# Destination rows of the second edge stage: spans of ranks and a selection on TensorE in place of gathers

## What is computed

```python
src_s = s @ msrc_ws                       # tables per node: TS
dst_s = s @ mdst_ws + mdst_bs             # and TD
ms = src_s[edge_src] + dst_s[edge_dst]    # scalars of an edge
mv = src_v[edge_src] + dst_v[edge_dst]    # vectors of an edge
...
a = jnp.exp(a - amax[edge_dst])           # a weight per edge and head
ns = jax.ops.segment_sum(vs * a[..., None], edge_dst, num_segments=n)
nv = jax.ops.segment_sum(vv * a[..., None, None], edge_dst, num_segments=n)
```

## Time and profile before

| what | value |
|---|---|
| median of 3 runs | 10502.52 us (10501.54 to 10524.19) |
| the profiled execution | 10505.42 us, span 10503.6 us |
| PE busy | 8641.0 us (82%) |
| DVE busy | 7996.0 us (76%) |
| POOL busy | 7636.1 us (73%) |
| ACT busy | 4717.1 us (45%) |
| mean granted TensorE clock | 0.923 of full |

### The profile page before, as it was taken

The page is one execution under the profiler, slowest core; times in us unless marked ns, Lnnn a source line. Parts: engine busy times, 40 slices in busy tenths (PEclk is TensorE's granted clock), DMA queues, the critical chain, the costliest instruction groups (busy, mean ns, idle before and its releaser), DMA issues. The chain is left out here.

```text
span 10503.6 us, 169632 instructions
## 1 busy us (share of the span) xinstructions
PE 8641.0 (82%) x31592; PEld 4931.7 (47%) x31592; DVE 7996.0 (76%) x15399; ACT 4717.1 (45%) x8484; POOL 7636.1 (73%) x5822
## 2 busy tenths in 40 slices
PE   0888888888888799999996888888888887788598
PEld 0444444444444232223233666666666665566333
DVE  3277777777777587888886888888888888888565
ACT  0177666666666311111112444444444444444255
POOL 4488888888888787777785777777777777777332
PEclk9599999999999899999997999999999999999699
DMA  5588888888888899999993444444444444444222
GB/s 202 177 169 168 166 167 166 169 164 172 165 167 168 180 231 225 228 226 229 228 226 90 136 138 136 135 133 139 136 135 135 136 140 135 133 135 137 71 76 58
DMA packets 1075659, 1661.68 MB, mean 158 GB/s; under 512 B 215917, under 2 KB 815288, under 8 KB 1019704
## 3 DMA queue, kind: packets, MB, share of 16 engines
q1 hardware_dynamic: 679744, 1199.16, 41.6%
q0 software_dynamic: 395520, 458.93, 24.5%
HBM read 1483.21 MB, written 443.97 MB: 183 GB/s over the span
## 5 line engine op out<-in xcount | busy, mean ns | idle before, releaser
L436 POOL DMA_INDIRECT sums<-e_total,e_place x1568 | 2481.9, 1583 | 586.3 <-DMA sums<-e_total,e_place 315.7
L1837 POOL DMA_INDIRECT e_rows<-TS,e_at x1568 | 1644.3, 1049 | 567.7 <-issue 451.4
L1837 POOL DMA_INDIRECT e_rows<-TD,e_at x1568 | 1537.3, 980 | 478.0 <-issue 478.0
L573 PE MATMUL ps<-e_win,e_pick 128*128 128x448 f32 x3136 | 1350.6, 576 | 152.9 <-DVE e_u L470 112.4
L1997 PE MATMUL ps<-w_r,e_h 128*128 128x224 f32 x3136 | 840.5, 420 | 424.6 <-DVE e_d L1880 376.1
L573 PEld LDWEIGHTS ps<-e_win,e_pick 128*128 128x128 f32 x3136 | 626.4, 205 | 920.0 <-issue 835.5
L1086 POOL TENSOR_TENSOR n_zv<-n_zv,n_ast 128x1536 f32<-128x1536 f32 x200 | 755.3, 3776 | 410.2 <-DMA n_zv<-in_x_groups 399.3
L1997 PEld LDWEIGHTS ps<-w_r,e_h 128*128 128x128 f32 x3136 | 659.2, 221 | 682.7 <-DVE e_d L1880 558.1
L2006 PE MATMUL ps<-ident,e_d 128*128 128x128 f32 x4704 | 683.6, 283 | 110.1 <-ACT e_dT L2114 108.6
L1266 PE MATMUL ps<-n_z,w_uss 128*64 128x512 f32 x1600 | 742.2, 607 | 26.5 <-DVE n_z L1109 25.8
L2114 ACT ACTIVATE e_oT<-ps 128x512 f32<-128x512 f32 x784 | 468.3, 597 | 628.3 <-PE ps L2032 488.5
(11 more groups left out here) (433 smaller groups left out, 18808.0 us busy)
## 6 DMA issues: line engine op xcount, KB each, us to landing
e_win<-T SPq DMA_DIRECT2D x1568, 168.0 KB
n_z<-in_x_groups SPq DMA_DIRECT2D x400, 512.0 KB
n_zv<-in_x_groups SPq DMA_DIRECT2D x800, 192.0 KB
TOT<-e_tot SPq DMA_DIRECT2D x392, 352.0 KB
e_row<-in_src_rows SPq DMA_DIRECT2D x98, 1024.0 KB
e_row<-in_dst_rows SPq DMA_DIRECT2D x98, 1024.0 KB
e_win<-T SPq DMA_DIRECT2D x1568, 56.0 KB
e_local<-LR SPq DMA_DIRECT2D x98, 512.0 KB
```

What stands on the lines that cost most here:

```text
L436: pool.indirect_dma_start(sums[c], bass.IndirectOffsetOnAxis(ap=place[:, r % 4, c:c + 1], axis=0), total[:, r % 4, c, 0:MSG0], None, compu ...
L573: pe.matmul(g[:, c, :], pick[:, p, R * c:R * c + R], win[:, s, c, :], start=True, stop=True).then_inc(spread, 1)
L1837: pool.indirect_dma_start(rows[:, p, x, c, :], None, table, bass.IndirectOffsetOnAxis(ap=at[:, gp, x, col:col + 1], axis=0)).then_inc(rows ...
```

## The change

TD is now stored by rank instead of by node number: in the node stage GpSimd scatters its rows (place, two scatters in each of the slots 6 and 7, with the rank numbers copied in slot 4), and SP stores only TS. TD gets 128 zero rows more, and baseI is stored to a table BASE, since the tile itself is gone by the second edge stage.

In the second edge stage:

- GpSimd gathers only TS: four indirect DMAs per group. After them it makes the selection e_pick for group i+1 from LR (512 columns, bf16 in, f32 out) and, for group i-8, the weighting e_val (640 columns), which VectorE did before.
- SP loads the windows, four groups ahead: per group eight register loads and eight DMAs on TD, four of them conditional.
- TensorE spreads group i+2: four products of 128 x 160, in two halves, into the two banks that the turns use. Both halves and both turn_backs now stand ahead of weights.
- ScalarE copies both halves (320 columns each) into e_rows.
- VectorE waits for these copies ahead of e_m, and no longer does the weighting.

```diff
-                sp.wait_ge(out_s, 16 * NB)
+                sp.wait_ge(based, 2)
+                sp.dma_start(BASE.rearrange("(a g) c -> a (g c)", a=1), baseI[:].rearrange("a g b c -> a (g b c)")).then_inc(out_s, 16)
+                sp.wait_ge(out_s, 16 * NB + 16)
...
-                    for j, to in enumerate((TS, TD)):
-                        sp.dma_start(to[at, :].rearrange("(t n) w -> n t w", t=2), rows[:, r, :, X * j:X * j + X]
-                                     ).then_inc(stored[r], 16)
+                    sp.dma_start(TS[at, :].rearrange("(t n) w -> n t w", t=2), rows[:, r, :, 0:X]).then_inc(stored[r], 16)
...
+                def ranks(c):
+                    if not c.before(2):
+                        for r in range(2):
+                            gate(pool, k)
+                            pool.wait_ge(placed[r], c.n(32, 0, 1))
+                    pool.tensor_copy(rank_of[:, c.p], rank[:, bass.ds(c.n(4), 4)]).then_inc(ranked, 1)
+
+                def place(c, r):
+                    gate(pool, k)
+                    pool.wait_ge(rows_kept, c.n(2, r + 1))
+                    gate(pool, k)
+                    pool.wait_ge(ranked, c.n(1, 1))
+                    pool.sem_inc(begun, 1)
+                    gate(pool, k)
+                    for j in range(2):
+                        pool.indirect_dma_start(TD, bass.IndirectOffsetOnAxis(ap=rank_of[:, c.p, 2 * r + j:2 * r + j + 1], axis=0),
+                                                rows[:, r, j, X:2 * X], None).then_inc(placed[r], 16)
+
                 def body(g):
                     for s in range(PARTS):
                         vectors(g, s)
                         if s == 1 and g.plus(1).within():
                             add_up(g.plus(1))
+                        if s == 4 and not g.before(1):
+                            ranks(g.plus(-1))
+                        if s >= 6 and not g.before(1):
+                            place(g.plus(-1), s - 6)
 
                 add_up(Group(0, 0))
                 groups(pool, body)
+                ranks(Group(NG // 2, 0))
+                for r in range(2):
+                    place(Group(NG // 2, 0), r)
...
-            return 2 + (5 * i.r + j) % 2
+            return 2 + (7 * i.r + j) % 2
...
+                def load_windows(i):
+                    s = i.r % 4
+                    if s == 0:
+                        sp.sem_inc(asked, 1)
+                        gate(sp, k)
+                        sp.wait_ge(base_here[i.r // 4], i.uses(16, 16))
+                    sp.sem_inc(asked, 1)
+                    gate(sp, k)
+                    _, starts = nc.values_load_multi_w_load_instructions(
+                        base[0:1, i.r // 4, s, 0:GT], engines=(mybir.EngineType.SP,),
+                        min_val=0, max_val=N - 1, skip_runtime_bounds_check_because="ranks count nodes, fewer than N")
+                    _, more = nc.values_load_multi_w_load_instructions(
+                        base[0:1, i.r // 4, s, GT:2 * GT], engines=(mybir.EngineType.SP,),
+                        min_val=0, max_val=1, skip_runtime_bounds_check_because="the outcome of a comparison")
+                    for c in range(GT):
+                        sp.dma_start(win[0:FEW, s, c, :], TD[bass.ds(starts[c], FEW), :]).then_inc(win_here[s], 16)
+                        sp.dma_start(win[FEW:128, s, c, :], TD[bass.ds(starts[c] + FEW, 128 - FEW), :], cond=more[c]
+                                     ).then_inc(win_here[s], 16)
...
-                        i = At(t, r)
+                        i, ahead = At(t, r), At(t, r).plus(4)
+                        if ahead.within():
+                            gate(sp, k)
+                            sp.wait_ge(spread, ahead.n(2, 2, 4))
+                            load_windows(ahead)
+                        if r % 4 == 0 and not final:
+                            load_base(r // 4, t + 1)
+                        if r % 4 == 1 and not final:
+                            gate(sp, k)
+                            sp.wait_ge(picked, i.n(1, 3))
+                            load_local(r // 4, t + 1)
...
+                def weighted(i, back):
+
+                    j = i.r - back
+                    slot, gp = j % STEPS, j % STEPS // 4
+                    gate(pool, k)
+                    pool.wait_ge(exped, i.uses(2, j // 4 + 1))
+                    u = val[:, gp, 4 * (slot % 4):4 * (slot % 4) + 4].rearrange("r c (h x) -> r (c h) x", x=SEG)
+                    pool.tensor_tensor(u[:, :, 1:SEG], u[:, :, 1:SEG], bc(u[:, :, 0], SEG - 1, 2), ALU.mult
+                                       ).then_inc(u_ready, 1)
+
+                def selections(i):
+
+                    p, s, gp = i.r % 2, i.r % 4, i.r // 4
+                    gate(pool, k)
+                    pool.wait_ge(local_here[gp], i.uses(16, 16))
+                    if not i.before(2):
+                        gate(pool, k)
+                        pool.wait_ge(spread, i.n(2, 2, 2))
+                    pool.sem_inc(begun, 1)
+                    gate(pool, k)
+                    pool.tensor_scalar(pick[:, p, :], local[:, gp, GT * R * s:GT * R * s + GT * R], iota[:, 0:1], None,
+                                      ALU.is_equal).then_inc(picked, 1)
...
-                        for x, table in enumerate((TS, TD)):
-                            for c in range(GT):
-                                col = 4 * (r % 4) + c
-                                pool.indirect_dma_start(rows[:, p, x, c, :], None, table, bass.IndirectOffsetOnAxis(
-                                    ap=at[:, gp, x, col:col + 1], axis=0)).then_inc(rows_here[p][x], 16)
+                        for c in range(GT):
+                            col = 4 * (r % 4) + c
+                            pool.indirect_dma_start(rows[:, p, 0, c, :], None, TS, bass.IndirectOffsetOnAxis(
+                                ap=at[:, gp, col:col + 1], axis=0)).then_inc(rows_here[p], 16)
+                        if i.plus(1).within():
+                            selections(i.plus(1))
+                        if not i.before(8):
+                            weighted(i, 8)
...
-                    for x in range(2):
-                        gate(dve, k)
-                        dve.wait_ge(rows_here[p][x], i.uses(256, 64 * (i.r // 2) + 64))
+                    gate(dve, k)
+                    dve.wait_ge(rows_here[p], i.uses(256, 64 * (i.r // 2) + 64))
+                    gate(dve, k)
+                    dve.wait_ge(far_kept, i.n(2, 2))
                     dve.tensor_tensor(m_[:, p], rows[:, p, 0], rows[:, p, 1], ALU.add).then_inc(added, 1)
...
-                        "r (c e) -> r c e", c=GT), bc(dstI[:, 0, bass.ds(i.n(4, 0, 5), GT)], R, 2), ALU.is_equal)
-                    gate(dve, k)
-                    dve.wait_ge(exped, i.uses(2, j // 4 + 1))
-                    u = val[:, gp, cols].rearrange("r c (h x) -> r (c h) x", x=SEG)
-                    dve.tensor_tensor(u[:, :, 1:SEG], u[:, :, 1:SEG], bc(u[:, :, 0], SEG - 1, 2), ALU.mult
-                                      ).then_inc(u_ready, 1)
+                        "r (c e) -> r c e", c=GT), bc(dstI[:, 0, bass.ds(i.n(4, 0, 5), GT)], R, 2), ALU.is_equal
+                                      ).then_inc(q_ready, 1)
...
+                def spread_out(i, half, to, after):
+                    p, s = i.r % 2, i.r % 4
+                    if half == 0:
+                        gate(pe, k)
+                        pe.wait_ge(picked, i.n(1, 1))
+                        gate(pe, k)
+                        pe.wait_ge(win_here[s], i.uses(256, 128 * (i.r // 4) + 128))
+                    if after is not None:
+                        gate(pe, k)
+                        pe.wait_ge(*after)
+                    for c in (2 * half, 2 * half + 1):
+                        last = pe.matmul(to[:, c % 2], pick[:, p, R * c:R * c + R], win[:, s, c, :], start=True, stop=True)
+                    last.then_inc(spread, 1)
...
+                        if i.plus(2).within():
+                            spread_out(i.plus(2), 0, far2(i, 0), (far_kept, 3) if i.before(1) else (kept, i.n(5, -1)))
+                        if not i.before(1):
+                            turn_back(i.plus(-1), 0)
+                        if i.plus(2).within():
+                            spread_out(i.plus(2), 1, far2(i, 1), (far_kept, 4) if i.before(1) else (kept, i.n(5)))
+                        if not i.before(1):
+                            turn_back(i.plus(-1), 1)
                         if not (isinstance(t, int) and t == PASSES - 1 and r == STEPS - 1):
                             weights(after)
-                        if not i.before(1):
-                            turn_back(i.plus(-1), 0)
-                            turn_back(i.plus(-1), 1)
...
+                def keep_far(i, half, of):
+                    gate(act, k)
+                    act.wait_ge(spread, i.n(2, half + 1))
+                    if half == 0 and not i.before(2):
```

(3 more changed lines are left out.)

98 lines of the change are left out of this document (73 added, 25 removed).

## The result

The changed kernel took **10799.8 us** (median of 4 runs, 10766.9 to 10801.7), the kernel before 10502.0 (4 runs, 10497.1 to 10524.2). The ratio is 1.028 with a 95% interval of 1.025 to 1.030: slower by some 300 us, where the forecast was 230 us faster and its range ended at 10560.

The account below looks back on a forecast made before the run. GpSimd was taken as the bound at 10.564 us per group, then VectorE at 9.93 (8.875 + 1.05): 248 us saved over 391 groups, 17 added, 231 in all, so about 10272 us; range 10060 to 10560.

Parts of the forecast that it names:

- dearer collision: Second edge stage: GpSimd's steps cost VectorE more than the forecast 1.05 us per group; with scatters showing, still faster: 0.13.
- The bound now, and VectorE behind it: Second edge stage: GpSimd's gathers and their issue fill the 10.564 us per group; VectorE is close behind.
- The selection, 0.75 us, between 0.53 and 1.27: GpSimd's new 512-column step per group, taken nearer a fill (0.53 us) than a two-input step (1.27 us).
- The weighting, 1.54 us: The 640-column step moved to GpSimd, priced at 2.12 ns per column from two two-input node-stage steps.
- The exclusion: GpSimd elementwise work and VectorE steps with two SBUF inputs exclude each other: 1.05 us lost per group, 0.4 to 2.0.
- VectorE without the weighting, 8.875 us: VectorE's own work per group of the second edge stage, averaged from three ordinary groups and one scan group.
- ScalarE "has room": Second edge stage: ScalarE gets two copies of 320 columns per group and has room; no cost given.
- TensorE second at 9.3: Second edge stage: TensorE needs 9.3 us per group with the four new products, 0.6 us under VectorE.
- The slower rival: GpSimd's two steps at their dear ends hold VectorE 2.0 us: 10.88 us per group, 10643 us; chance of slower 0.19.
- Queues and ends: SP's window loads (4.70 us per group) delay nothing; the second edge stage's start costs 6 us, its end 3 us.
- The node stage, +8: GpSimd's four TD scatters per node group, mostly hidden by its lead, add 8 us; ends 0 and 127.

Follow-up runs that it names:

- e5_again: The changed kernel with GpSimd's selection made for only the first of a group's four tiles (128 of 512 columns): 10465.7 us, 321 us less than the unaltered changed kernel.
- e1_again: The changed kernel with ScalarE's exponential and its table loads ahead of the two copies, nothing else changed: 10585.1 us, 201 us less than the unaltered changed kernel.
- after_again: The changed kernel once more, unaltered, as control in a later session: 10786.7 us, 1.026 times the kernel before beside it.
- c_before: The kernel before, unaltered, executed once in a later session: 10477.0 us.

## Why the prediction was wrong

The profiled execution took 10798.0 us where 10274.4 was forecast, 523.6 more. 484 of these are in the second edge stage's period, 11.167 us instead of 9.93: 0.39 for a dearer collision (1.44 instead of 1.05), 0.57 for ScalarE's order, 0.25 for VectorE's own work, 0.03 open. 24 are in the node stage and 23 ahead of it, and the ends of the stage took 8 less. By the prediction's own sum the dearer collision alone, 152 us, would have left the change faster, at 10424; it is with the other two that it became slower.

**The bound now, and VectorE behind it.** Right: with the TD gathers gone GpSimd had time to spare (its part was forecast as 7.9 us, and it idles 2.8 of 11.2), and VectorE's clock took over.

**The selection, 0.75 us, between 0.53 and 1.27.** This is the first step that failed. It takes 1.59 us, outside both bounds. By e5_again, where 0.97 us of selection cost 0.84 us a group, the missing 0.84 us cost about 0.73 a group or 290 us, an estimate; the collision came out only 0.39 too dear by luck, since the weighting was priced too high and many groups lose less than the one that was walked through. The fill of 512 columns was taken for a neighbour because only one stream is read; but the step converts bf16 to f32 and compares against a pointer operand, and the prediction itself named both as unseen on this engine. With no row for the operation, the upper bound was a row of another operation and not a bound. Which of type, operand and operation makes it 1.59 us, no run separates. The Trainium skill's best case for a loop of 512 elements ("GPSIMD Engine Reference", section 3.1, 769 ns) is half of what the row shows, and the one-input work that section 4.1 calls roughly line-rate was not cheaper than two-input work here: 1.59 us for 512 columns against 1.27.

**The weighting, 1.54 us.** Too dear by 0.29: 1.255 measured, though its runs are 20 columns long.

**The exclusion.** The mechanism was right, to the place: the comparison and the mask held to the weighting's end. It was incomplete: not the comparison alone but in 48 of 223 groups the silu step ahead of it, and the hold begins within the selection. By the prediction's own arithmetic, with gathers to T+6.5, 1.6 and 1.26 us, the weighting ends at T+9.4 and the comparison loses 1.6 us instead of 1.05. The mean over groups is 1.44, silu step included. The Trainium skill's rule that the loser is fully blocked ("SBUF — State Buffer", Who interferes with whom) agrees with the weighting's rows and only in part with the selection's, where 45 comparisons beside it lost nothing and other steps at most 0.6 us. Of the 1.44, 0.84 go with the selection's length (e5_again).

**VectorE without the weighting, 8.875 us.** Too low by 0.25: the mean of before is 9.13, as shown above. Two groups were taken for four, and neither of the two was the one behind the scans, where the kernel before already waits for ScalarE. By the prediction's rule the change turns slower not from 1.65 us lost per group on but from 1.39.

**ScalarE "has room".** The second step that failed, and it wasn't priced at all. Its busy share, 47%, is low as foreseen; what counts is order. The two copies were put ahead of the exponential, which VectorE waits for through its values, and they come late themselves. The copies' wait, the exponential and two table loads cost VectorE 0.57 us per group more than before, 223 us. e1_again gives 201 us back with the order alone.

**TensorE second at 9.3.** In order of rank right, never the bound: it waits for the scans. The 1.5 us at the half clock are named there and not in the 9.3; with them it is 9.65. The best variants run at 9.93, so the floor isn't tested below that.

**The slower rival.** It came true in direction and in its first part. It needed 1.65 us lost through the exclusion, and that took 1.44; the other 0.57 came from ScalarE, which it did not have. With the exclusion alone and VectorE's true 9.13 a group would have taken 10.57 us, what it took before. It was given 0.19 because two rows agree on a rate (L1090 and L1086), but both are two-input products, and the rival was about a conversion.

**Queues and ends.** SP waits for no window, and behind the start nobody waits for one: right. TensorE waits 62.2 us for the first window, in a start that is hardly longer than before: it cost 0.9 us (103.8 us from the last n_zv to the first L1966, 102.9 before) and the end 0.5, against 6 and 3.

**The node stage, +8.** It is 2014.7 us from first to last n_zv against 1982.6: +32; in other sessions 1997.6 (after_again) against 1972.6 (c_before), +25. The same code took 1979 to 2017 us in the traces of all changed kernels, so +32 is near the upper end of a wide spread. Inside its 0 to 127, up to four times the value taken. The scatters wait for ScalarE's rows and the vectors behind them with them:

```profile
POOL TD L1115 <- ACT n_rows L1522: 130.1, 17, 13.1
POOL n_zv L1094 <- DMA n_zv<-in_x_groups: 112.4, 33, 8.2
```

That is 3560 to 5560 us; the second row was 399.3 us before. So most of the lead that GpSimd had was used up rather than all of the cost hidden.

**What was in no term.** The first edge stage, whose code isn't changed, is 29 us longer. Its 1568 scatters take at least 1548 to 1556 ns instead of 1537, in every changed kernel's trace and in neither of the kernel before: 13 ns x 1568 = 20 us in the changed kernel. Why is open. Of the 29 us 23 are left where the node stage begins.
